# Five VectorE instructions for a pair of steps instead of ten, in the delta-rule recurrence of the first layer

## The reference, cut to what matters

```python
def _step(Sm, inputs):
    q_t, k_t, v_t, beta_t = inputs
    Sk = jnp.einsum('bhde,bhe->bhd', Sm, k_t)
    delta = v_t - Sk
    Sm = Sm + beta_t[..., None] * jnp.einsum('bhd,bhe->bhde', delta, k_t)
    o_t = jnp.einsum('bhde,bhe->bhd', Sm, q_t)
    return (Sm, o_t)
```

## Time and profile before

| what | value |
|---|---|
| time, median of 3 runs | 5192.89 us (5187.05 to 5199.76) |
| time of the profiled execution | 5190.3 us |
| its span, first to last instruction | 5188.7 us |
| mean granted TensorE clock | 0.906 |
| DVE busy over the span | 3570.5 us |
| recurrence of the first layer | 63.14 to 495.12 us of the span |

### The profile page before, as it was taken

One profiled execution on the slowest core, in us unless ns is written; L12 is line 12 of the kernel. 1 busy time (PEld: TensorE's weight loads), 2 busy tenths in 40 slices (PEclk: granted clock), 3 DMA queues, 4 the chain that ended last, 5 costly groups with the idle time before them and its releaser, 6 DMA issues. The chain is left out here.

```text
span 5188.7 us, 47328 instructions
## 1 busy us (share of the span) xinstructions
PE 4065.8 (78%) x13734; PEld 1854.4 (36%) x13734; DVE 3570.5 (69%) x4968; ACT 2530.8 (49%) x3913; POOL 2856.4 (55%) x2181
## 2 busy tenths in 40 slices
PE   7999527982956988888887798997789777777776
PEld 2444203750423653333332444543333222222222
DVE  7998426121545759999998644444443699999999
ACT  5553311330445876666665244444346555555554
POOL 3776451027034439999996301113331489988997
PEclk8999759995977999999999899988889899999999
DMA  1100200211111115444443333321110343334443
GB/s 48 51 35 35 76 33 25 68 52 53 55 74 48 58 50 169 155 153 153 155 153 110 86 45 40 43 40 40 32 41 17 109 137 135 133 134 140 136 135 102
DMA packets 161701, 434.82 MB, mean 84 GB/s; under 512 B 28151, under 2 KB 51385, under 8 KB 160049
## 3 DMA queue, kind: packets, MB, share of 16 engines
q1 hardware_dynamic: 142512, 374.41, 23.8%
q0 software_dynamic: 18944, 57.57, 3.2%
HBM read 363.67 MB, written 68.68 MB: 83 GB/s over the span
## 5 line engine op out<-in xcount | busy, mean ns | idle before, releaser
L1680 ACT ACTIVATE mb_h<-m_dt,m_a_neg 128x512 f32<-128x512 f32 x1024 | 665.0, 681 | 725.8 <-DVE r L1835 332.9
L1539 PE MATMUL mb_y<-r,m_diag_y 128*128 128x512 f32 x1024 | 549.3, 671 | 273.0 <-POOL r L1760 164.6
L1826 DVE TENSOR_TENSOR_SCAN mb_h<-mb_h,m_u 128x1024 f32<-128x1024 f32 x320 | 733.9, 2294 | 10.8 <-DVE mb_h L1815 0.5
L1783 POOL TENSOR_TENSOR m_u<-m_bsb,m_xs 128x1024 f32<-128x1024 f32 x256 | 600.2, 2369 | 175.7 <-DMA m_bsb<-bc_rows 175.7
L1783 POOL TENSOR_TENSOR m_u<-m_bsb,m_dtx 128x1024 f32<-128x1024 f32 x256 | 596.0, 2359 | 50.9 <-DVE m_dtx L1867 28.2
L1539 PE MATMUL mb_y<-m_hc,w_common 128*128 128x512 f32 x1024 | 499.6, 628 | 149.5 <-DVE m_hc L1835 84.6
L1826 DVE TENSOR_TENSOR_SCAN m_hs<-mb_h,m_u 128x1024 f32<-128x1024 f32 x192 | 437.6, 2279 | 1.7 <-POOL m_u L1783 1.7
L1539 PEld LDWEIGHTS mb_y<-r,m_diag_y 128*128 128x128 f32 x1024 | 196.3, 207 | 621.0 <-POOL r L1760 245.3
L2309 DVE TENSOR_REDUCE at_mx<-at_ps_s 128x4 f32<-128x512 f32 (+1 forms) x256 | 243.2, 957 | 235.2 <-PE at_ps_s L2123 235.1
L1760 POOL TENSOR_TENSOR r<-m_hs,m_csb 128x1024 f32<-128x1024 f32 x128 | 308.2, 2408 | 118.0 <-DVE m_hs L1826 117.4
L1539 PEld LDWEIGHTS mb_y<-m_hc,w_common 128*128 128x128 f32 x1024 | 191.5, 197 | 449.2 <-issue 195.0
(11 more groups left out here) (518 smaller groups left out, 8584.9 us busy)
## 6 DMA issues: line engine op xcount, KB each, us to landing
m_bsb<-bc_rows SPq DMA_DIRECT2D x256, 512.0 KB, 4.9
m_csb<-bc_rows SPq DMA_DIRECT2D x256, 512.0 KB, 4.0
at_q<-q_parts SPq DMA_DIRECT2D x144, 128.0 KB
x_slots<-d_zeros SPq DMA_DIRECT2D x8, 1024.0 KB, 5.1
kept_x<-r SPq DMA_DIRECT2D x2, 4096.0 KB
xg_xg<-x_slots SPq DMA_DIRECT2D x32, 256.0 KB
y_slots<-xg_yo POOLq DMA_DIRECT2D x32, 256.0 KB
xl_xg<-x_slots SPq DMA_DIRECT2D x32, 256.0 KB
```

The source lines that it names most:

```text
L1539: mm = nc.tensor.matmul(ps_y[:, h], weight, hc[:, q % RING, s], start=False, stop=g == GROUPS - 1 and s == SG - 1)
L1680: ins = nc.scalar.activation(ps_h[:, q % 2, s], dt[:, i % 2, h], ACT.Exp, scale=a_neg[:, n:n + 1])
L1783: nc.gpsimd.tensor_tensor(u[:, q % RING], bsb[:, n % RING], dtx[:, i % 2, h].unsqueeze(1).broadcast_to([P, SG, TILE]), ALU.mult).then_inc( ...
L1826: V.tensor_tensor_scan(flat(to), flat(ps_h[:, q % 2]), flat(u[:, q % RING]), 0.0, ALU.mult, ALU.add).then_inc(h_ready, 1)
```

## The change

The two halves are done by one instruction, for each of the five operations. The access patterns get the half as an outer dimension, the semaphores are raised by 2, and each instruction waits for the full count.

```diff
-                for f in range(2):
-                    dve.wait_ge(state_ready, 2 * n + f + 1)
-                    V.tensor_tensor(prod[:, part, p % (PAIRS // 2), f, :, 0:D0], old[:, at[f]].unsqueeze(1).broadcast_to([P, 2, HS]),
-                                    kb_up[:, i % 2, p, f].rearrange("p (sh e) -> p sh e", e=D0).unsqueeze(2)
-                                    .broadcast_to([P, 2 * HH, D0, D0]), ALU.mult).then_inc(stepped, 1)
-                for f in range(2):
-                    dve.wait_ge(stepped, n * 8 + f + 1)
-                    V.tensor_reduce(upd[:, f], prod[:, part, p % (PAIRS // 2), f], AX, ALU.add).then_inc(stepped, 1)
-                for f in range(2):
-                    dve.wait_ge(stepped, n * 8 + f + 3)
-                    V.tensor_tensor(outer[:, f], upd[:, f].unsqueeze(2).broadcast_to([P, HALF, D0]),
-                                    k2[:, i % 2, p, f].rearrange("p (sh e) -> p sh e", e=D0).unsqueeze(2)
-                                    .broadcast_to([P, 2 * HH, D0, D0]), ALU.mult).then_inc(stepped, 1)
+                dve.wait_ge(state_ready, 2 * n + 2)
+                halves = lambda ap: ap.rearrange("p (f c) -> p f c", f=2)
+                V.tensor_tensor(prod[:, part, p % (PAIRS // 2)].rearrange("p f c e -> p (f c) e")[:, :, 0:D0],
+                                halves(old).unsqueeze(2).broadcast_to([P, 2, 2, HS]),
+                                kb_up[:, i % 2, p].rearrange("p f (sh e) -> p (f sh) e", e=D0).unsqueeze(2)
+                                .broadcast_to([P, 4 * HH, D0, D0]), ALU.mult).then_inc(stepped, 2)
+                dve.wait_ge(stepped, n * 8 + 2)
+                V.tensor_reduce(upd, prod[:, part, p % (PAIRS // 2)], AX, ALU.add).then_inc(stepped, 2)
+                dve.wait_ge(stepped, n * 8 + 4)
+                V.tensor_tensor(outer[:].rearrange("p f (c e) -> p (f c) e", e=D0),
+                                upd.rearrange("p f c -> p (f c)").unsqueeze(2).broadcast_to([P, 2 * HALF, D0]),
+                                k2[:, i % 2, p].rearrange("p f (sh e) -> p (f sh) e", e=D0).unsqueeze(2)
+                                .broadcast_to([P, 4 * HH, D0, D0]), ALU.mult).then_inc(stepped, 2)
                 if n >= 3:
                     dve.wait_ge(sq_ready, n - 2)
-                for f in range(2):
-                    dve.wait_ge(stepped, n * 8 + f + 5)
-                    V.tensor_tensor(one[:, at[f]], old[:, at[f]], outer[:, f, 0:HS], ALU.subtract).then_inc(stepped, 1)
-                for f in range(2):
-                    dve.wait_ge(stepped, n * 8 + f + 7)
-                    V.tensor_tensor(two[:, at[f]], one[:, at[f]], outer[:, f, HS:], ALU.subtract).then_inc(state_ready, 1)
+                dve.wait_ge(stepped, n * 8 + 6)
+                V.tensor_tensor(halves(one), halves(old), outer[:, :, 0:HS], ALU.subtract).then_inc(stepped, 2)
+                dve.wait_ge(stepped, n * 8 + 8)
+                V.tensor_tensor(halves(two), halves(one), outer[:, :, HS:], ALU.subtract).then_inc(state_ready, 2)
```

More of the change, by code:

```diff
@@ L593, in pair @@
                 old, one, two = state[:, (n + 2) % 3, 1], state[:, n % 3, 0], state[:, n % 3, 1]
-                at = [slice(f * HS, (f + 1) * HS) for f in range(2)]
                 part = (2 * i + p // (PAIRS // 2)) % 3
-                for f in range(2):
-                    dve.wait_ge(state_ready, 2 * n + f + 1)
-                    V.tensor_tensor(prod[:, part, p % (PAIRS // 2), f, :, 0:D0], old[:, at[f]].unsqueeze(1).broadcast_to([P, 2, HS]),
-                                    kb_up[:, i % 2, p, f].rearrange("p (sh e) -> p sh e", e=D0).unsqueeze(2)
-                                    .broadcast_to([P, 2 * HH, D0, D0]), ALU.mult).then_inc(stepped, 1)
```

## The result

The changed kernel is slower: 5261.0 us median (5252.0 to 5270.0, 4 runs) against 5195.2 (5187.1 to 5199.8), a ratio of 1.0129 with the 95% interval [1.011, 1.0148]. That is +66 us; forecast were 5231, which is +38, and a range of 5216 to 5246. The profiled execution took 5269.97 us, its span 5268.3, some 80 us more than the profiled execution before (5188.7); the medians, 66 apart, are the fairer comparison.

The account below looks back on a forecast made before the run. DVE was taken to bound the recurrence alone. A pair going from 2.835 to 3.198 us gives +46.5 us over 128 pairs, with -8.9, +1.1 and -0.2 making +38.5: 5231 us, range 5216 to 5246.

Parts of the forecast that it names:

- what bounds the stage, and that nothing absorbs the loss: DVE, busy 429.75 of 431.98 us, alone sets the recurrence's length; what a pair loses, 128 times, the kernel loses.
- merged durations: Lengths forecast for a pair's five merged DVE instructions: 0.681, 0.752, 0.692 and twice 0.414, together 2.953 us.
- the exposed tail: In the merged pair on DVE, nothing may start under the last 0.083 us of an instruction whose successor waits for it.
- the 75 places with an inserted operation: Between pairs, an independent DVE operation follows the last L616, sparing overlap and gap: 75 x 0.118 = -8.9 us.
- four gaps of 0.035 and one of 0.105: Gaps behind a merged pair's five DVE instructions, the long one ahead of the first subtraction (L613): 0.245 us a pair.
- Rival A: On DVE waits cost nothing, only the instruction count matters; faster, 5176 us as PE limits the gain; chance 0.05.
- Rival C: PE's granted clock drops in the recurrence, PE comes to bound: +30 us, 5261; chance 0.06, shared with slower merged access patterns.
- The merged forms at less than a column a cycle: Merged access patterns on DVE run slower, 512-column forms lasting well over 0.70 us; shares rival C's chance of 0.06.
- Rival B: No change, 5193 us: the merged pair costs as before if exposed tail and gap together were only 0.06 us; chance 0.05.
- bounds of the forecast: 5221 to 5243: L612's separate wait costing no extra, -9.8; inserted operations taking nothing back, +8.9; PSUM writes, +5 us.

## Why the prediction was wrong

**Right: what bounds the stage, and that nothing absorbs the loss.** What the pairs lost arrived in the stage, and the stage's +73.8 us in the whole within the spread of the runs (+66, and +70 on the other chip). The merged durations came within 0.01 us each except the product (0.669 for 0.681); together 2.974 for 2.953, +2.7 us over 128 pairs.

**Right: the exposed tail.** An operation that waits for the one in front starts 0.035 us after its end, an independent one 0.08 before it. The run with unmerged halves in turn shows it without any wide instruction, the 75 places with an inserted operation show it inside the changed kernel (L613 at 310.41 lasts to 310.83, L583 starts at 310.75).

**Wrong: "four gaps of 0.035 and one of 0.105".** That step took every wait to be carried as in the kernel before, and overlooked that the diff also changes `then_inc(stepped, 1)` to 2. Here no instruction that raises by 2 carries a wait. Three gaps in a pair grew by 0.07 and the one ahead of the first subtraction by 0.03: (3 x 0.07 + 0.03) x 128 = 31 us. Of the 52 products that follow a subtraction directly, 37 that I had priced at 0.035 took 0.104: +2.6. With the durations: 38.5 + 31 + 2.6 + 2.7 = 74.8, against 73.8 measured. That it closes within 1 us is partly luck: left out are terms that in part cancel, the largest of them the add of `inverse`, which in the first two tiles of the kernel before came early and lasted long, and no longer does (-3.5), and the four single delays (+1.4). The run with raises by 1 and the predecessor's wait first gives the size of all that separate waits cost: its stage, 468.5, is 37.5 us shorter, although the steps to and from L577 took 15.2 us there and 8.5 in the changed kernel, and the whole falls to +33. Its stage is 36.3 us above the 432.2 of before, near the +38.5 forecast for waits that are carried; 5 of the 36.3 are the stretched add, which the forecast didn't have.

**Rival A** (waits cost nothing, the number of instructions counts) fell in every run: ten instructions beat five, and the same ten in another order cost 123 us more. The Trainium skill, "VectorE: DVE Perf Modes", section "The DRAIN you can't avoid", quoted with it, says that a wait between VectorE copies costs nothing, as the pipeline empties anyway; it adds that a next operation that isn't held starts earlier, which the prediction left out. (The advice to keep down the number of operations stands in another section of that page, "Rules for kernel authors".) The traces agree with the addition (0.08 us of overlap for an independent one) and not with the rest where the second instruction needs the first: 0.118 us each, and 0.19 where the wait is separate.

**Rival C.** PE's granted clock did fall, from 0.98 to 0.91 over the stage, and PE's busy time rose from 405.75 to 427.16 us. But C needed a mean clock under 0.88 in the stage, and POOL no longer waited for PE at all where it had waited 13 times: in a longer stage PE has the room. All of L525's waits are for DVE (total us, times, longest):

```profile
POOL d_sq_q L525 <- DVE d_state L613: 172.0, 84, 4.7
```

That C's number, 5261, is the measured one to the microsecond is chance: nothing of its mechanism is in the trace. The merged forms at less than a column a cycle, which shared its chance, are excluded by the durations above. **Rival B** (no change) is excluded by the pair of 3.53 us, and by one of 3.15 even where the waits are carried.

**Slips in the sums.** The bounds of the forecast add up to 5245 (5231 + 8.9 + 5), not 5243, and its chance together with C's to 0.90, not 0.89. Neither changes the forecast.

**What stays open.** That the raise is the cause is shown (the run with raises by 1 restores the gap). Why no instruction has both, and whether the chip or the compiler decides it, was not measured; the traces only show that none has. Which other instructions wait so for GpSimd wasn't tried, nor whether the form or the operand in PSUM frees the add. What the single delays are stays open too.

## What to carry to other kernels

Before merging alternating halves of a chain on VectorE into wide instructions, count the places where an instruction then waits for the one directly in front: each cost 0.12 to 0.13 us here (0.08 of lost overlap, 0.035 of gap), while an instruction saved is worth 0.06. Merge only where an independent instruction of enough length stands on either side. Raise a semaphore by 1 from an instruction that also waits, and name the wait for the nearest predecessor first; a raise by 2 cost 34 us of the 74 in this change without doing anything.

## What the runs showed that I had not expected

- An instruction that raised its semaphore by 2 never carried a wait; 640 waits moved to the sequencer, and the gap behind a predecessor's end went from 0.035 to 0.104 us; two such waits in one sequencer instruction (50 ns) made it 0.133.
- A 64-column TENSOR_SCALAR with all operands in SBUF took 0.18 to 0.20 us, or 0.45 to 1.29 where it started while a GpSimd operation was running. That happened 41 times in the recurrences of the traces with this form, and each time it ended 0.05 us behind that operation. The reciprocal behind it, also from SBUF to SBUF, kept to its 0.55 us beside a running GpSimd operation. In the run with raises by 1 the stretched add cost 10 us of the stage by nothing but an unlucky phase against L525, more than the order of two waits. As a `tensor_tensor` with the constant in PSUM it took 0.21 to 0.23 us each time.
- The unchanged kernel took 4915 and 4908 us on two chips and 5191 to 5195 on the others; its instructions are the same. The changed kernel, for which there are traces of both kinds of chip, lies 295 us apart on them, and some 240 of these come up in the second layer, where on the slower chip DVE stood still for up to 27 us at a time while GpSimd issued its indirect DMAs. The cause wasn't looked into.
